# Stretches of scores exchanged and the split of the score maxima moved to GpSimd, in a float32 attention and feed-forward kernel

## The chip, the cores and the metric

The kernel runs on one core of one Trainium2 chip. The metric is the device time of one execution in microseconds (us); less is better. Engines: PE (TensorE), DVE (VectorE), ACT (ScalarE), POOL (GpSimd), SP (SyncE, which here issues nearly all DMAs).

## The reference

Two sequences of T = 1024 rows of D = 512 pass attention with 32 query heads and 8 key/value heads of 16 columns, a layer norm, a gated feed-forward layer with 1408 hidden columns, and a second layer norm, in float32:

```python
Q, K = _rope(x @ Wq.T + bq), _rope(x @ Wk.T + bk); V = x @ Wv.T + bv   # by heads
w = softmax(einsum('bhqd,bhkd->bhqk', Q, K) / sqrt(16))
x = _layernorm(x + einsum('bhqk,bhkd->bhqd', w, V) @ Wo.T + bo)
hdn = silu((x @ gate_w.T) * gate_s) * ((x @ up_w.T) * up_s)
x = _layernorm(x + (hdn @ down_w.T) * down_s)
```

## The kernel before

The main loop runs over iterations u, written (n, v) with u = 16n + v. n is one of 16 pairs of batch and key/value head, v counts 2 halves of the queries (qh) times 8 tiles of 128 keys (kt). A group is the 8 iterations of one n and qh. In each iteration the four query heads g of the key/value head have their scores computed for 128 keys and 512 queries (`scores`, L448, PE into one of three PSUM banks PS2), ACT takes the exponential of each (`exponent`, L756), and one iteration later `weigh` (L467) multiplies the exponentials with the values into the bank PV, eight matmuls on four column groups. A bank of PS2 is free when its exponential is done. After 8 iterations ACT copies PV to SBUF (`finish`, L765) and SP sends it to DRAM (L1524); the next group's first `weigh` waits for that copy.

Behind each score PE issues half a step of the running maxima for a later group (`maxima_half`, L426, on other rows of the array than the score), into one of two slots of two banks in PSA. DVE reduces them (`maximum`): for g = 2 and 3 both halves at once (L964, 128x1024), for g = 0 and 1 half by half (L957, L960). Two steps fall to one iteration. With the last of a group's 16 steps, in iteration 3 or 11 of an n, `turn_max` runs four small instructions on DVE: join of the halves (L973), a rounded copy (L977), the remainder (L979), a 32x32 transposition (L984). SP's `write_max` waits for it, writes the result to DRAM (`mscr`, L1511), waits for that to land, and reads it back as two more rows of the operand Qt (L1514). The first score of the group 5 iterations later waits for this read.

`weigh(u - 1)` comes after g = 2 in even iterations and after g = 3 in odd ones. So five scores lie between two of them, then three. The first score behind the `weigh` of an even iteration (c % 8 == 3) is split into pieces of 128 and 384 columns.

Other work is tied to iteration numbers by tables: `project_at` (projection of one 128-row block of Q or K, 24 matmuls, L365), `values_at`, `out_at` (output projection, L493), each after the scores of an odd iteration, 11 in all, in the two banks that `free_banks` names; `rope_end` (ACT rounds one half, L748, POOL subtracts, L1286, SP writes the block out); `recip_at` (DVE reciprocal L990, SP writes it, L1541, and, when that has landed, reads it back spread over partitions, 512 KB, `Bn<-rscr`, L1547, then POOL multiplies, L1330); `gather_at` (the twelve DMAs that fetch Qt and Kt of head n + 2). Every engine runs its own program in order; SP takes in iteration u first `write_max`, then `finish`, `swap_halves` (L1477, L1478), the reciprocal's two transfers, and later entries. Those of `recip_at` at (2, 11), (4, 11), (6, 3), (8, 3) and (10, 3) share their iteration with a turn of the maxima. The last 12 iterations and the feed-forward layer follow in `feed_forward`.

## Time and profile before

| what | value |
|---|---|
| runs, median of 3 | 1063.52 us (1063.1 to 1064.48) |
| profiled execution | 1064.13 us, its span 1062.3 us |
| PE busy | 1026.5 us (97%), granted clock 0.998 |
| DVE, ACT, POOL busy | 809.5, 665.1, 266.2 us |
| exponentials (L756) | 1146, mean 559 ns |
| maxima (L964, L960, L957) | 256 each, mean 1219, 682, 681 ns |

The span runs from the first to the last instruction of the program; the execution's own time has 1.8 us around it. Times in the rows below are counted from the start of the span. Mean durations overlap the next instruction's start, so what an instruction costs its engine is read from start to start. A digit of busy share says little here, because the end of a matmul is modelled.

### The profile page before, as it was taken

Reading aid. Unit: us, or ns where it says so; the run is one execution under the profiler, and the core shown is the slowest. Engines: PE = TensorE matmul, PEld = TensorE weight load, DVE = VectorE, ACT = ScalarE, POOL = GpSimd, SP = SyncE. Lnnn points to the kernel's source line nnn. Section 1 sums busy time; section 2 is a strip of 40 time slices with the busy share of each in tenths; the row PEclk is TensorE's granted clock in tenths of the full one; section 3 lists DMA queues with packets and bytes.
Section 4 is the critical chain, followed back from the end, with each engine's and each line's share of the span. In section 5 each row is a group of like instructions: output and inputs, shape, how many; then the busy total and the mean of one; then the engine's idle time right before and its main releaser. Section 6 shows DMA issues by size and latency. Waiting matters only on the chain.

```text
span 1062.3 us, 15699 instructions
## 1 busy us (share of the span) xinstructions
PE 1026.5 (97%) x5858; PEld 536.8 (51%) x5858; DVE 809.5 (76%) x1199; ACT 665.1 (63%) x1346; POOL 266.2 (25%) x227
## 2 busy tenths in 40 slices
PE   8999999999999999999999999999999999999996
PEld 3643344433443433443444443333337888888885
DVE  4899978899779799779988899999803475662535
ACT  2368877788778788778766678888863431222221
POOL 2751030141335422246200042844100000000002
PEclk9999999999999999999999999999999999999999
DMA  5274417243142512344140446531217510402011
GB/s 200 80 196 126 106 35 213 52 97 78 52 115 75 105 56 54 82 108 105 34 78 12 116 120 150 124 121 37 93 68 193 166 40 9 111 28 52 1 39 42
DMA packets 64432, 94.87 MB, mean 89 GB/s; under 512 B 37536, under 2 KB 37920, under 8 KB 62272
## 3 DMA queue, kind: packets, MB, share of 16 engines
q1 hardware_dynamic: 63776, 93.10, 33.2%
q8 instruction: 48, 0.79, 0.3%
q10 hardware_dynamic: 576, 0.72, 0.2%
q14 instruction: 32, 0.26, 0.1%
HBM read 53.95 MB, written 27.00 MB: 76 GB/s over the span
## 4 chain that ended last, share of the span: by engine, by line
PE 80%; DVE 10%; ACT 6%; issue 2%; DMA 1%; SPq 0%; POOL 0%; DVEq 0%; POOLq 0%
PE PS L448 21%; PE PV L467 20%; PE PSA L537 15%; PE PS L554 5%; PE PSA L426 5%; DVE nmx L964 5%; PE PS L365 4%; ACT Bn L756 3%; PE PS L493 2%; PE PSA L493 2%; DVE nmx L960 2%; DVE nmx L957 2%; ACT Bn L765 2%; PE PV L554 2%; PE PSA L365 1%
## 5 line engine op out<-in xcount | busy, mean ns | idle before, releaser
L756 ACT ACTIVATE Bn<-PS 128x512 f32<-128x512 f32 x1146 | 548.8, 559 | 125.0 <-PE PS L448 111.1
L448 PE MATMUL PS<-Qt,Kt 50*128 50x512 f32 x1146 | 391.7, 434 | 20.0 <-ACT Bn L756 18.7
L426 PE MATMUL PSA<-Kt,Qt 48*128 48x512 f32 x1024 | 390.0, 459 | 2.2 <-DVE Kt L936 0.8
L964 DVE TENSOR_REDUCE nmx<-PSA 128x1 f32<-128x1024 f32 x256 | 312.2, 1219 | 61.0 <-PE PSA L426 59.8
L448 PEld LDWEIGHTS PS<-Qt,Kt 50*128 50x128 f32 x1146 | 184.4, 184 | 323.6 <-ACT Bn L756 312.7
L467 PE MATMUL PV<-Bn 128*32 128x512 f32 x2048 | 272.8, 605 | 0.0
L426 PEld LDWEIGHTS PSA<-Kt,Qt 48*128 48x128 f32 x1024 | 174.6, 183 | 21.7 <-DVE nmx L964 6.2
L960 DVE TENSOR_REDUCE nmx<-PSA 128x1 f32<-128x512 f32 x256 | 174.5, 682 | 1.4 <-PE PSA L426 1.1
L957 DVE TENSOR_REDUCE nmx<-PSA 128x1 f32<-128x512 f32 x256 | 174.3, 681 | 0.0
L537 PE MATMUL PSA<-x1Th,wr 128*128 128x512 f32 x344 | 135.0, 393 | 0.8 <-DVE sg L1052 0.5
L537 PE MATMUL PSA<-x1Tl,wr 128*128 128x512 f32 x344 | 134.7, 392 | 0.0
L1052 DVE SCALAR_TENSOR_TENSOR sg<-PSA,us,sg 128x512 f32<-128x512 f32 x43 | 32.1, 749 | 103.8 <-ACT sg L792 103.8
L792 ACT ACTIVATE sg<-PSA,gs 128x512 f32<-128x512 f32 x43 | 29.6, 690 | 128.3 <-PE PSA L537 128.2
L467 PEld LDWEIGHTS PV<-Bn 128*32 128x32 f32 x2048 | 40.3, 108 | 75.8 <-issue 75.8
L537 PEld LDWEIGHTS PSA<-x1Th,wr 128*128 128x128 f32 x344 | 64.6, 188 | 16.9 <-issue 1.8
L537 PEld LDWEIGHTS PSA<-x1Tl,wr 128*128 128x128 f32 x344 | 64.6, 188 | 14.8 <-issue 1.5
L1351 POOL TENSOR_SCALAR ve<-mv 128x2 f32<-128x2 f32 (+1 forms) x11 | 2.9, 260 | 263.9 <-DVE mv L999 263.9
L1278 POOL TENSOR_TENSOR A<-A 128x1024 f32<-128x1024 f32 x8 | 19.1, 2382 | 174.4 <-DMA A<-A 172.6
L1330 POOL TENSOR_TENSOR Bn<-Bn 128x1024 f32<-128x1024 f32 x8 | 19.1, 2385 | 148.4 <-DMA Bn<-rscr 148.4
L1072 DVE TENSOR_TENSOR hTl<-sg,hTh 128x512 fp32r<-128x512 f32 x38 | 26.3, 693 | 31.8 <-ACT hTh L805 31.8
L805 ACT CAST hTh<-sg 128x512 fp32r<-128x512 f32 x38 | 23.6, 621 | 42.8 <-DVE sg L1052 36.8
L554 PE MATMUL PS<-wr,hTh 128*128 128x512 f32 x114 | 44.6, 391 | 0.0
(166 smaller groups left out, 919.4 us busy)
## 6 DMA issues: line engine op xcount, KB each, us to landing
Qt<-pscr SPq DMA_DIRECT2D x90, 128.0 KB, 4.9
A<-in_wf SPq DMA_DIRECT2D x11, 768.0 KB, 6.3
wr<-A SPq DMA_DIRECT2D x33, 256.0 KB, 2.9
pscr<-A SPq DMA_DIRECT2D x16, 512.0 KB, 3.7
vscr<-Bn SPq DMA_DIRECT2D x32, 256.0 KB, 2.0
Kt<-pscr SPq DMA_DIRECT2D x90, 64.0 KB, 2.3
A<-A SPq DMA_DIRECT2D x16, 256.0 KB, 3.7
Bn<-vscr SPq DMA_DIRECT2D x8, 512.0 KB
```

The lines of the kernel that those rows point to most:

```text
L365: op = e.matmul(ps, v, t, start=first and i == 0, stop=last and end)
L426: op = e.matmul(PSA[:, 2 * s + h, :], Qt[n % 3][p:p + NC_, g % 2, 128 * qt:128 * qt + 128], Kt[n % 3][p:p + NC_, 512 * h:512 * h + 512], s ...
L448: e.matmul(PS2[:, i, cols], Kt[n % 3][rows, 128 * kt:128 * kt + 128], Qt[n % 3][rows, g % 2, 512 * qh + cols.start:512 * qh + cols.stop], ...
L467: op = e.matmul(PV[32 * g:32 * g + 32, :], Bn[:, o:o + 32], Pb[c % NP_], start=(kt == 0), stop=(kt == 7), tile_position=(0, 32 * g))
L493: op = e.matmul(ps, t_, v, start=(k == 0 and i == 0), stop=(k == KT - 1 and i == len(pairs) - 1))
L537: op = e.matmul(gate_bank(x, q, j), v, t, start=(k == 0 and m == 0), stop=(k == KT - 1 and m == (1 if x else 0)))
L554: op = e.matmul(bank(t), v, t_, start=(i == 0 and m == 0), stop=(i == FI - 1 and end))
L756: e.activation(Pb[c % NP_][:, cols], PS2[:, score_bank[c, p], cols], ACT.Exp, scale=0.25).then_inc(*act_exp.next(piece(c, p)))
L957: e.tensor_reduce(nmx[:, hh % 2, 16 + c0:17 + c0], slot_pair(s)[:, 0, :], AX.X, ALU.max, negate=True).then_inc(*dve_max[s].next((k, 0)))
L960: e.tensor_reduce(nmx[:, hh % 2, c0:c0 + 1], slot_pair(s)[:, 1, :], AX.X, ALU.max, negate=True).then_inc(*dve_max[s].next(k))
L964: e.tensor_reduce(nmx[:, hh % 2, c0:c0 + 1], slot_pair(s), AX.XY, ALU.max, negate=True).then_inc(*dve_max[s].next(k))
L1052: e.scalar_tensor_tensor(out=out, in0=gate_bank(x, q, 1), scalar=us[:, i:i + 1], in1=sg[q % 2], op0=ALU.mult, op1=ALU.mult).then_inc(*dve_ ...
```

## The change

The order of `weigh` is exchanged: after g = 3 in even iterations and after g = 2 in odd ones, and the split score moves with it to c % 8 == 7. Projection, value and output stages now follow directly on the `weigh` of an odd iteration, ahead of its fourth score; ACT's evacuations and DVE's additions are put at the same place in their programs. For groups 1 to 30 (`apart`) DVE keeps the join, POOL does the rounded copy and the remainder (`split_max`), and DVE transposes after the first maximum of the next group. SP writes the maxima in iteration 4 of 8 instead of 3, behind what it issues in iteration 3. The fetch of head n + 2 moves from (n, 3) to (n, 5), and the roundings come 7 and 9 iterations after a projection instead of 6 and 7.

```diff
--- before.py
+++ after.py
@@ -250,6 +250,7 @@
         dve_gate, dve_h, dve_x, dve_z = count("dve_gate"), count("dve_h"), count("dve_x"), count("dve_z")
         dve_out, dve_turn, dve_parts = count("dve_out"), count("dve_turn"), count("dve_parts")
 
+        pool_ms = count("pool_ms")
         pool_one, pool_cs, pool_rope = count("pool_one"), count("pool_cs"), count("pool_rope")
         pool_split, pool_xb, pool_at = count("pool_split"), count("pool_xb"), count("pool_at")
         pool_low, pool_ve, pool_add = count("pool_low"), count("pool_ve"), count("pool_add")
@@ -262,15 +263,15 @@
         jobs = [(0, 1), (0, 2), (0, 3), (1, 4), (1, 0), (1, 1), (1, 2), (1, 3)]
         project_at = {(1, 11): 2, (4, 11): 3, (5, 3): 4, (6, 3): 5, (8, 3): 6, (8, 11): 7}
         rope_end = {(0, 1): (0, "h0"), (0, 2): (0, "h1"), (0, 3): (0, "out"),
-                    (0, 4): (1, "rope"), (0, 7): (1, "h0"), (0, 9): (1, "h1"), (0, 10): (1, "out")}
+                    (0, 4): (1, "rope"), (0, 8): (1, "h0"), (0, 10): (1, "h1"), (0, 11): (1, "out")}
         for at_u, j in project_at.items():
-            u0 = 16 * at_u[0] + at_u[1] + 6
-            rope_end.update({divmod(u0, 16): (j, "h0"), divmod(u0 + 1, 16): (j, "h1"), divmod(u0 + 2, 16): (j, "out")})
+            u0 = 16 * at_u[0] + at_u[1] + 7
+            rope_end.update({divmod(u0, 16): (j, "h0"), divmod(u0 + 2, 16): (j, "h1"), divmod(u0 + 3, 16): (j, "out")})
         values_at = (2, 11)
         out_at = {(10, 3): 0, (10, 11): 1, (11, 3): 2, (11, 11): 3}
         norm_at = {(10, 11): 0, (11, 3): 1, (11, 11): 2}
         recip_at = {(2, 11): 0, (4, 11): 1, (6, 3): 2, (8, 3): 3, (10, 3): 4, (12, 6): 5, (14, 6): 6}
-        gather_at = {(n, {0: 13, 6: 5}.get(n, 3)): n + 2 for n in range(NG - 2)}
+        gather_at = {(n, {0: 13}.get(n, 5)): n + 2 for n in range(NG - 2)}
         x_at = {(part // 2, 8 * (part % 2)): (0, part) for part in range(4)}
         x_at.update({(2 + part // 2, 5 + 8 * (part % 2)): (1, part) for part in range(4)})
         ffn_at, low_at = {}, {}
@@ -286,12 +287,19 @@
 
             return stream[k][2] < 2
 
+        def apart(hh):
+
+            return 1 <= hh < 2 * NG - 1
+
+        def low_max(hh):
+            return (pool_ms if apart(hh) else dve_ms).at(("low", hh))
+
         def slot_pair(s):
             return PSA[:, 2 * s:2 * s + 2, :]
 
         def pieces(c):
 
-            return [slice(0, 128), slice(128, 512)] if c % 8 == 3 and c < 4 * SPLIT else [slice(0, 512)]
+            return [slice(0, 128), slice(128, 512)] if c % 8 == 7 and c < 4 * SPLIT else [slice(0, 512)]
 
         score_bank = {}
         for c in range(4 * U):
@@ -302,7 +310,7 @@
             return c if p == len(pieces(c)) - 1 else (c, p)
 
         def free_banks(u):
-            last = score_bank[4 * u + 3, len(pieces(4 * u + 3)) - 1]
+            last = score_bank[4 * u + 2, 0]
             return (last + 1) % 3, last
 
         def ffn_slots(x):
@@ -663,6 +671,20 @@
                     project_half(1, 0, 0, (1, 2, 3))
                 else:
                     project_half(1, 1, 3, ((0, 1), (2, 3))[k - 2])
+            def background(u):
+                at_u, pair = divmod(u, 16), free_banks(u)
+                if at_u in project_at:
+                    for h, i in enumerate(pair):
+                        project_half(project_at[at_u], h, i, (0, 1, 2, 3))
+                if at_u == values_at:
+                    for t in range(8):
+                        value_rows(1, t, pair[t // 4])
+                if at_u in out_at:
+                    t2 = out_at[at_u]
+                    out_project(False, 0, t2, [bank(i) for i in pair], [bank_free[i] for i in pair])
+                    for j, i in enumerate(pair):
+                        bank_free[i] = dve_y.at((False, 0, 2 * t2 + j))
+
             for u in range(SPLIT):
                 at_u = divmod(u, 16)
                 for g in range(4):
@@ -670,19 +692,9 @@
                     advance(1)
                     if len(pieces(4 * u + g)) == 2:
                         scores(u, g, 1)
-                    if u >= 1 and g == (2, 3)[u % 2]:
+                    if u >= 1 and g == (3, 2)[u % 2]:
                         weigh(u - 1)
-                if at_u in project_at:
-                    for h, i in enumerate(free_banks(u)):
-                        project_half(project_at[at_u], h, i, (0, 1, 2, 3))
-                if at_u == values_at:
-                    for t in range(8):
-                        value_rows(1, t, free_banks(u)[t // 4])
-                if at_u in out_at:
-                    t2, pair = out_at[at_u], free_banks(u)
-                    out_project(False, 0, t2, [bank(i) for i in pair], [bank_free[i] for i in pair])
-                    for j, i in enumerate(pair):
-                        bank_free[i] = dve_y.at((False, 0, 2 * t2 + j))
+                        background(u)
                 if at_u == (15, 1):
                     flag_sum()
                 if at_u == (15, 2):
@@ -892,11 +904,11 @@
                 at_u = divmod(u, 16)
                 for g in range(4):
                     exponent(u, g)
+                    if g == 2 and at_u in project_at:
+                        for h, i in enumerate(free_banks(u)):
+                            evacuate_raw(project_at[at_u], h, i)
                 if u >= 1:
                     finish(u - 1)
-                if at_u in project_at:
-                    for h, i in enumerate(free_banks(u)):
-                        evacuate_raw(project_at[at_u], h, i)
                 if at_u in rope_end and rope_end[at_u][1] in ("h0", "h1"):
                     round_half(rope_end[at_u][0], int(rope_end[at_u][1] == "h1"))
                 if at_u == (15, 2):
@@ -944,33 +956,40 @@
                     bv[:, :].rearrange("p (o v c) -> p o v c", o=1, v=NKV).to_broadcast([128, 4, NKV, HD]),
                     ALU.add).then_inc(*dve_val.next((b, h)))
 
-            def maximum(k):
+            def maximum(k, halves=(0, 1)):
                 if k >= len(stream):
                     return
                 s, hh = slot_of(k), k // 16
                 g, qt = stream[k][2], stream[k][1]
                 c0 = 4 * g + qt % 4
                 if hh >= 2:
-                    w.wait_ge(*dve_ms.at(("low", hh - 2)))
+                    w.wait_ge(*low_max(hh - 2))
                 if by_halves(k):
-                    w.wait_ge(*pe_max.at((k, 0)))
-                    e.tensor_reduce(nmx[:, hh % 2, 16 + c0:17 + c0], slot_pair(s)[:, 0, :], AX.X, ALU.max, negate=True).then_inc(
-                        *dve_max[s].next((k, 0)))
-                    w.wait_ge(*pe_max.at(k))
-                    e.tensor_reduce(nmx[:, hh % 2, c0:c0 + 1], slot_pair(s)[:, 1, :], AX.X, ALU.max, negate=True).then_inc(
-                        *dve_max[s].next(k))
+                    for h in halves:
+                        w.wait_ge(*pe_max.at((k, 0) if h == 0 else k))
+                        col = nmx[:, hh % 2, c0 + 16 * (h == 0):c0 + 16 * (h == 0) + 1]
+                        e.tensor_reduce(col, slot_pair(s)[:, h, :], AX.X, ALU.max, negate=True).then_inc(
+                            *dve_max[s].next((k, 0) if h == 0 else k))
                 else:
                     w.wait_ge(*pe_max.at(k))
                     e.tensor_reduce(nmx[:, hh % 2, c0:c0 + 1], slot_pair(s), AX.XY, ALU.max, negate=True).then_inc(
                         *dve_max[s].next(k))
-                if k % 16 == 15:
-                    turn_max(hh)
-
-            def turn_max(hh):
+                if 1 in halves and k % 16 == 15:
+                    join_max(hh)
+                    if not apart(hh):
+                        split_max(hh)
+                        turn_max(hh)
+                if k % 16 == 0 and k > 16 and apart(hh - 1):
+                    turn_max(hh - 1)
+
+            def join_max(hh):
                 top, rest = nmx[:, hh % 2, 0:16], nmx[:, hh % 2, 16:24]
                 for k in (16 * hh + 14, 16 * hh + 15):
                     w.wait_ge(*dve_max[slot_of(k)].at(k))
                 e.tensor_tensor(top[:, 0:8], top[:, 0:8], rest, ALU.min).then_inc(*dve_ms.next(("join", hh)))
+
+            def split_max(hh):
+                top = nmx[:, hh % 2, 0:16]
                 w.wait_ge(*dve_ms.at(("join", hh)))
                 if hh >= 1:
                     w.wait_ge(*dve_ms.at(("turn", hh - 1)))
@@ -978,7 +997,9 @@
                 w.wait_ge(*dve_ms.at(("high", hh)))
                 e.tensor_tensor(msp[:, 16:32], top, msp[:, 0:16].bitcast(F32), ALU.subtract).then_inc(
                     *dve_ms.next(("low", hh)))
-                w.wait_ge(*dve_ms.at(("low", hh)))
+
+            def turn_max(hh):
+                w.wait_ge(*low_max(hh))
                 if hh >= 2:
                     w.wait_ge(*max_out[hh % 2].at(hh - 2))
                 e.transpose(mrow[:, hh % 2, :], msp[:, :].bitcast(F32)).then_inc(*dve_ms.next(("turn", hh)))
@@ -1216,14 +1237,19 @@
             for u in range(SPLIT):
                 at_u = divmod(u, 16)
                 maximum(next(steps))
-                maximum(next(steps))
-                if at_u in norm_at:
-                    first_norm(False, 0, norm_at[at_u])
-                if at_u == values_at:
-                    for h, i in enumerate(free_banks(u)):
-                        add_values(1, h, i)
-                if at_u in out_at:
-                    add_rows(False, 0, out_at[at_u], [bank(i) for i in free_banks(u)])
+                k = next(steps)
+                if at_u in norm_at or at_u in out_at or at_u == values_at:
+                    maximum(k, (0,))
+                    if at_u in norm_at:
+                        first_norm(False, 0, norm_at[at_u])
+                    if at_u == values_at:
+                        for h, i in enumerate(free_banks(u)):
+                            add_values(1, h, i)
+                    if at_u in out_at:
+                        add_rows(False, 0, out_at[at_u], [bank(i) for i in free_banks(u)])
+                    maximum(k, (1,))
+                else:
+                    maximum(k)
                 if at_u in recip_at:
                     reciprocal(recip_at[at_u])
                 if at_u == (15, 0):
@@ -1266,6 +1292,15 @@
                     w.wait_ge(*act_split.at(("x0", h, k)))
                     e.tensor_tensor(xl0[j][:, :], xT[:, h, k, :], xh0[j][:, :].bitcast(F32), ALU.subtract).then_inc(
                         *pool_split.next(("x0", h, k)))
+
+            def split_max(hh):
+                top = nmx[:, hh % 2, 0:16]
+                w.wait_ge(*dve_ms.at(("join", hh)))
+                w.wait_ge(*dve_ms.at(("turn", hh - 1)))
+                e.tensor_copy(msp[:, 0:16], top).then_inc(*pool_ms.next(("high", hh)))
+                w.wait_ge(*pool_ms.at(("high", hh)))
+                e.tensor_tensor(msp[:, 16:32], top, msp[:, 0:16].bitcast(F32), ALU.subtract).then_inc(
+                    *pool_ms.next(("low", hh)))
 
             def rope(j):
                 b, m = jobs[j]
@@ -1410,6 +1445,8 @@
                 at_u = divmod(u, 16)
                 if at_u in norm_at:
                     spread_of(2, (False, 0, norm_at[at_u]))
+                if u % 8 == 3 and apart(steps_done(u) // 16 - 1):
+                    split_max(steps_done(u) // 16 - 1)
                 if at_u in project_at:
                     rope(project_at[at_u])
                 if at_u in recip_at:
@@ -1653,8 +1690,10 @@
             swap_halves(1)
             for u in range(SPLIT):
                 at_u = divmod(u, 16)
-                if steps_done(u) // 16 > steps_done(u - 1) // 16:
+                if u % 8 == 4:
                     write_max(steps_done(u) // 16 - 1)
+                if u == SPLIT - 1:
+                    write_max(2 * NG - 1)
                 if u >= 1:
                     finish(u - 1)
                 if at_u in project_at:
```

## Rows read from the trace of the kernel before

**Rows 1.** the page's part 4, the chain that ended last, by engine

```profile
PE 80%; DVE 10%; ACT 6%; issue 2%; DMA 1%; SPq 0%; POOL 0%; DVEq 0%; POOLq 0%
```

**Rows 2.** timeline of PE, two periods (start us, length us, engine, line, operation, count)

```profile
221.08 1.06 PE L467 MATMUL PV<-Bn 128*32 128x512 f32 x8
...
224.61 1.06 PE L467 MATMUL PV<-Bn 128*32 128x512 f32 x8
...
226.50 1.06 PE L467 MATMUL PV<-Bn 128*32 128x512 f32 x8
...
229.55 1.06 PE L467 MATMUL PV<-Bn 128*32 128x512 f32 x8
...
231.44 1.06 PE L467 MATMUL PV<-Bn 128*32 128x512 f32 x8
...
234.90 0.64 PE L467 MATMUL PV<-Bn 128*32 128x512 f32 x4
```

**Rows 3.** timeline of ACT, same stretch (in brackets: idle before it, releaser)

```profile
223.04 0.58 ACT L765 COPY Bn<-PV 128x512 f32<-128x512 f32 x1
...
226.14 4.40 ACT L756 ACTIVATE Bn<-PS 128x512 f32<-128x512 f32 x9 [0.54 <-PE PS L448]
```

**Rows 4.** timeline of DVE, around one turn of the maxima

```profile
228.75 1.23 DVE L964 TENSOR_REDUCE nmx<-PSA 128x1 f32<-128x1024 f32 x1
...
230.49 0.68 DVE L960 TENSOR_REDUCE nmx<-PSA 128x1 f32<-128x512 f32 x1
231.28 0.17 DVE L973 TENSOR_TENSOR nmx<-nmx 128x8 f32<-128x8 f32 x1
...
232.03 1.18 DVE L964 TENSOR_REDUCE nmx<-PSA 128x1 f32<-128x1024 f32 x1
```

**Rows 5.** timeline of ACT, two roundings of a half

```profile
67.68 0.64 ACT L748 CAST A<-A 128x512 fp32r<-128x512 f32 x1
...
70.68 0.61 ACT L748 CAST A<-A 128x512 fp32r<-128x512 f32 x1
```

**Rows 6.** timeline of all engines, copy of PV in the tail

```profile
772.70 1.06 PE L467 MATMUL PV<-Bn 128*32 128x512 f32 x8
...
773.83 0.59 ACT L765 COPY Bn<-PV 128x512 f32<-128x512 f32 x1 [0.43 <-PE PV L467]
774.31 1.09 ACT L756 ACTIVATE Bn<-PS 128x512 f32<-128x512 f32 x2
```

**Rows 7.** groups of instructions on GpSimd (count | busy us, mean ns | idle before)

```profile
L1291 POOL TENSOR_TENSOR xl<-A,xh 128x512 fp32r<-128x512 f32 x8 | 10.3, 1284 | 0.6
...
L1351 POOL TENSOR_SCALAR ve<-mv 128x2 f32<-128x2 f32 x2 | 0.5, 237 | 35.4 <-DVE mv L999 35.4
```

**Rows 8.** timeline of PE, end of a projection stage

```profile
277.29 0.39 PE L365 MATMUL PS<-xl,wh 128*128 128x512 f32 x1
...
278.88 1.06 PE L467 MATMUL PV<-Bn 128*32 128x512 f32 x8
```

**Rows 9.** timeline of SP's issues, iterations (4, 11) and after

```profile
273.43 0.57 SPq L1511 DMA_DIRECT2D mscr<-mrow  x1
275.41 0.54 SPq L1514 DMA_DIRECT2D Qt<-mscr  x2
...
279.64 0.59 SPq L1541 DMA_DIRECT2D rscr<-rn  x1
282.86 0.66 SPq L1547 DMA_DIRECT2D Bn<-rscr  x1
```

**Rows 10.** busy time by stretch (each engine, PE clock, DMA share, GB/s)

```profile
285.00:287.00 2.00, 2.00 (x15) 0.97 (x19) 2.00 (x3) 1.85 (x6) 2.00 (x2) 1.00 0.51 147
288.50:289.50 1.00, 1.00 (x12) 0.16 (x8) 0.84 (x2) 1.00 (x3) 1.00 (x1) 1.00 0.02 8
```

**Rows 11.** timeline of SP's issues, the latest read of the maxima

```profile
656.51 0.56 SPq L1511 DMA_DIRECT2D mscr<-mrow  x1
662.81 0.56 SPq L1514 DMA_DIRECT2D Qt<-mscr  x2
```

## The prediction

> **What bounds the kernel now.** I read the page first. PE looks busy nearly all the time, and the chain of waits puts 80% of the span on PE, 10% on DVE and 6% on ACT [rows 1]. That is no proof that PE is the limit, because matmul ends are modelled. So I went to PE's timeline in a quiet piece of the attention loop, and read the starts of the value product (L467, called W here; eight matmuls, about 1.0 us until the next one can start) [rows 2]. They alternate. From W at 224.61 to W at 226.50 is a short stretch of 1.89 us (three scores), from 226.50 to 229.55 a long one of 3.05 us (five scores, the first in two pieces). Two iterations take 4.94 us.
>
> In ACT's view [rows 3] nine exponentials run without a gap for 4.40 us, and ACT idles 0.54 us ahead of them, which is where W has kept PE from giving it a score. In the long stretch PE waits for banks that ACT empties, so work put on ACT there costs its full time. In the gap behind the long stretch's W, ACT has 0.54 us to give away. DVE [rows 4] starts a whole-pair maximum at 228.75 and the second half maximum after it at 230.49. With 0.60 us to whatever may follow, one iteration of maxima is 2.34 us and two are 4.68, which leaves 0.26 us of slack. ACT sets the pace, with DVE close behind.
>
> Three kinds of place depart from 4.94:
> - Copy of PV (L765), once in eight iterations, in the long stretch: 221.08 to 224.61 is 3.53 us, 0.48 more [rows 2, 3]. The loop has 30 such stretches of 3.53 or 3.54.
> - Four small DVE instructions (L973 to L984): the next maximum starts at 232.03 instead of 230.49 + 0.60 = 231.09, 0.94 us late. The long stretch of that moment, 231.44 to 234.90, has 3.46 us, 0.41 more [rows 2, 4]. There are 14 of these. The others lie beside a projection stage, or behind a stretch in which DVE had caught up, and cost nothing.
> - Rounding a half (L748): at 67.68 it lies in ACT's gap and costs nothing. At 70.68 it lies between exponentials of a long stretch and costs about 0.5 [rows 5]. Seven lie so.
>
> **The change, part by part.** *Exchange of stretches.* By itself it is a shift by one iteration, so 4.94 stays. What is tied to iteration numbers moves against it. The copy of PV stays at the end of iteration 8m, which now is where the long stretch's W ends, in ACT's gap. The nearest row is in the tail, where the copy waits for its W: W 772.70, copy 773.83, next exponential 774.31 [rows 6]. So the exponential comes at W + 1.61, where ACT's gap ends at W + 1.53 (229.55 to 231.08, the start behind the nine, 226.14 + 4.40 + 0.54). Those 0.08 us vanish in the 0.15 that ACT idles ahead of the split score. Gain: 30 x 0.48 = **14.4 us**. The next W needs the copy's end at W + 1.72 and comes at W + 1.89: 0.17 to spare.
>
> *Roundings.* Both halves now fall behind even iterations, in the gap. Two keep a cost: (0, 1), now in a long stretch, and (0, 8), which meets the copy. From seven to two: 5 x 0.5 = **2.5 us**.
>
> *Maxima.* DVE keeps the join and the transposition. The join still waits for the last maximum: 231.28 - 230.49 = 0.79, then about 0.13 to an instruction that doesn't depend on it, less the 0.60 of before: 0.32. The transposition comes a maximum later, when nothing is left to wait for: 0.13 [rows 4]. So DVE loses 0.45 instead of 0.94 us, in two parts. Against 0.26 of slack in two iterations it is caught up in the next two. Followed maximum by maximum, the slots come free 0.01 to 0.05 us ahead of the matmuls that want them. So most of 14 x 0.41 = **5.7 us** is gained, and I take back **1.0** for these thin margins (bounds 0 and 30 x 0.41 = 12.3, if every turn stalls as the 14 did).
>
> *The split on GpSimd.* No row has 16 columns. The bounds are 0.24 us (128x2) and 1.28 (128x512) for each of the two [rows 7]. I take 0.3, as both are nearly all start-up, plus two semaphores: ready 0.7 us after the join. The transposition comes 1.14 + 0.1 after it, the length of a whole-pair maximum, so this is hidden. GpSimd's long work (the rotation, the splits of x, w and A, the low parts) starts behind the split in program order and takes at most some 15 us of the 19.8 between two splits. [...]
>
> *Projection, value and output stages*, 11 of them, go between W and the split score. Before, last product 277.29 to W 278.88 is 1.59, and a long stretch of 3.05 follows [rows 8]: 4.64. After, a short stretch of 1.89 precedes the stage, and behind it the second evacuation, the two-piece score, three exponentials and four scores take about 2.8 us to W: 4.7. I cost it at nothing. DVE's last half maximum and the join now come behind the stage, but its next maximum waits for PE anyway.
>
> *Rows fetched later.* The twelve issues of a gather go from iteration 3 to 5, behind the write of the maxima, still 14 iterations ahead of their use: nothing.
>
> *Write of the maxima.* This is what speaks against the change. SP's write (L1511) goes from iteration 8m+3 to 8m+4, and so is moved past everything that SP issues at 8m+3. Normally it is issued at 273.43, read back from 275.41 [rows 9], and the read has about 1.5 us more to land, by an estimate from the write's own 1.98, of which it has half the bytes; with 0.3 for the second issue that makes 3.8 us. The new turn leaves 7.3 us to the first score that needs it (8.7 before), so it is hidden in ordinary groups. In five groups, however, the reciprocal's write and the broadcast read RB (L1547, 512 KB) stand at 8m+3 as well. Count from the last product of the stage, E = 277.29. The reciprocal is written at E + 2.35 (279.64), and RB is issued at E + 5.57 (282.86) [rows 8, 9]. Now the write of the maxima follows, at E + 6.2. RB keeps half of the DMA engines busy (share 0.51 at 285 to 287) and is over by 288.5 to 289 (0.02 left) [rows 10]. That small writes wait for large transfers issued ahead is in the trace: the write at 656.51 lets its read go only at 662.81, 6.3 us instead of 1.98 [rows 9, 11]. So it lands near E + 12, and the maxima near E + 13.9. PE wants them at 2.8 + 4.94 + 1.9 + 1.3 = E + 10.9: PE stands for 3.0 us, of which a fuller ring of banks gives 0.1 back. That is three groups, (4,11), (6,3), (8,3): **8.7 us**. At (2,11) and (10,3) no swap of halves delays the reciprocal's write and RB goes out 1.5 us sooner: 2 x 1.3 = **2.6**. The group of the late write at 656.51 had only 0.5 us left, and its transfers don't speed up while PE does by 1.6: **1.1**. Sum 12.4; bounds 0 (the write isn't held up) and 18 (RB as slow as with a gather beside it, 2 us more in three).
>
> The Trainium skill (DMA: Bandwidth & Descriptors, Why a DMA increments its semaphore by 16 and not by 1, and Queues, rings and completion order) says that such a transfer uses only the k lowest-numbered engines and that each consumes descriptors in ring order. The half share agrees. By that rule the case half way in rival 1 is the right one.
>
> **Sum.** -14.4 - 2.5 - 5.7 + 1.0 + 12.4 = -9.2. The profiled execution has 1064.1 us (span 1062.3 and 1.8 around it), which gives 1054.9. The median of the runs is 0.6 lower, so 1063.5 - 9.2 = **1054.3 us**.
>
> **Rivals.**
> 1. *The write isn't held up* (other engines, or RB drains sooner). For it: I know its engines by no row. Against: 656.51. Without the 12.4: 1042; with a third of it, 1046. Chance 0.17. Half way lies the case in which the write waits for its own few engines alone: one us less in each of five groups gives 1050, the lower end of my own range, and has 0.15 of the chance of my forecast.
> 2. *DVE becomes the limit at each turn.* For it: margins of hundredths. Against: 0.45 of added work, not 0.94. If half of the 12.3 comes: 1060. The same size follows if W has to wait 0.2 us for the copy of PV in 30 places. Chance 0.14.
> 3. *Slower: GpSimd is late.* The upper bound for the pair is 2.6 us. If it costs 2.0, the transposition holds DVE for 0.8 us, and what is beyond its slack, about 0.6, stops PE in 30 groups: +18, so 1072. It decides once the pair takes over 1.24 + 0.25 + 0.3 = 1.8 us. Chance 0.08.
> 4. *Gains and stalls cancel* (copy saves half, stalls at their upper bound): 1063. Chance 0.06.
>
> My forecast has 0.55, with 1050 to 1059 as its own range. The range 1044 to 1061 takes in most of 1 and 2 and leaves the rest. A difference under 0.2% (2 us) is about what a measurement of this kernel can't tell from none. Faster 0.85, within 0.2% 0.06, slower 0.09.
>
> **What the profile will show.** Right: L765 behind a gap on ACT at W + 1.1, and no stretch of 3.5 left; L748 behind it; the transposition between two maxima with no gap; GpSimd's pair under 0.7 us; and in five groups SP's L1511 straight behind L1547, its read 5 to 6 us later, and PE standing some 3 us at the first score of the next group. Wrong: the write of the maxima taking 2 us even there (rival 1), long stretches of 3.2 or more behind each turn (2), or DVE idle ahead of the transposition with GpSimd as releaser (3).

## The result, and the profile after

| kernel | median | runs |
|---|---|---|
| before | 1063.37 us | 4 |
| after | 1077.07 us (1074.61 to 1079.0) | 4 |

The changed kernel is slower: ratio 1.0126, 95% interval 1.0103 to 1.0148. The forecast was 1054.3 us with a range of 1044 to 1061 and 0.09 for slower; the time lies 22.8 us above it and outside the range. The profiled execution of after took 1077.6 us, span 1075.7, granted clock 0.98.

Begin with what came as forecast. PE's timeline of after, at the place of [rows 2]; W is now L475:

```profile
218.48 1.06 PE L475 MATMUL PV<-Bn 128*32 128x512 f32 x8
...
221.52 1.07 PE L475 MATMUL PV<-Bn 128*32 128x512 f32 x8
...
223.41 1.07 PE L475 MATMUL PV<-Bn 128*32 128x512 f32 x8
...
226.45 1.06 PE L475 MATMUL PV<-Bn 128*32 128x512 f32 x8
```

The steps are 3.04, 1.89 and 3.04. The stretch of 3.53 is gone, although the copy of PV lies right here. ACT's timeline shows why, against [rows 3]:

```profile
218.12 4.39 ACT L768 ACTIVATE Bn<-PS 128x512 f32<-128x512 f32 x9 [0.54 <-PE PS L456]
222.65 0.59 ACT L777 COPY Bn<-PV 128x512 f32<-128x512 f32 x1
223.13 4.30 ACT L768 ACTIVATE Bn<-PS 128x512 f32<-128x512 f32 x9
```

The copy starts at 222.65, 1.13 behind W at 221.52, in the gap that ACT had there, and the nine exponentials behind it follow without a gap. The turn of the maxima, in the timelines of DVE and of GpSimd (POOL), against [rows 4]:

```profile
230.77 0.17 DVE L989 TENSOR_TENSOR nmx<-nmx 128x8 f32<-128x8 f32 x1
230.86 1.22 DVE L975 TENSOR_REDUCE nmx<-PSA 128x1 f32<-128x1024 f32 x1
231.99 0.20 DVE L1005 STREAM_TRANSPOSE mrow<-msp 128x32 f32<-128x32 f32 x1
```

```profile
231.00 0.20 POOL L1300 CAST msp<-nmx 128x16 fp32r<-128x16 f32 x1 [10.35 <-DVE nmx L989]
231.28 0.22 POOL L1302 TENSOR_TENSOR msp<-nmx,msp 128x16 fp32r<-128x16 f32 x1
```

GpSimd is done at 231.50, 0.5 us ahead of the transposition, which stands between two maxima with no idle time. In heads 1 to 14 no stretch of 3.46, 3.53 or 3.56 is left in after; the only longer ones lie in projection, value and output stages and in the six places below.

What went wrong shows first in the chain of waits by engine, against [rows 1]. DVE and ACT, 16% before, have nearly left it, and transfers have come in:

```profile
PE 85%; DMA 8%; DVE 3%; ACT 1%; SPq 1%; issue 1%; POOL 0%; DVEq 0%; POOLq 0%
```

Then in PE's waits, by releaser (line waited for: us in total, times, longest):

```profile
PE PS L456 <- DMA Qt<-mscr: 15.2, 5, 4.0
PE PSA L434 <- DVE nmx L971: 7.2, 1, 7.2
```

The five are the five groups of the forecast: 2.63 us at 199.03, 3.01 at 288.48, 4.00 at 366.55, 4.04 at 458.35, 1.54 at 552.48. SP's issues around the second, against [rows 9]:

```profile
276.67 0.59 SPq L1578 DMA_DIRECT2D rscr<-rn  x1
279.89 0.64 SPq L1584 DMA_DIRECT2D Bn<-rscr  x1
280.62 0.58 SPq L1548 DMA_DIRECT2D mscr<-mrow  x1
286.25 0.57 SPq L1551 DMA_DIRECT2D Qt<-mscr  x2
```

The write of the maxima stands straight behind the read RB, and its own read goes 5.63 us later instead of 1.98 (5.63 to 6.25 in the five groups). The forecast had 5 to 6. What it did not have stands at each wait. PE's timeline:

```profile
288.48 0.76 PE L456 MATMUL PS<-Qt,Kt 50*128 50x512 f32 x1 [3.01 <-DMA Qt<-mscr]
...
290.66 1.93 PE L475 MATMUL PV<-Bn 128*32 128x512 f32 x8
...
294.10 1.37 PE L475 MATMUL PV<-Bn 128*32 128x512 f32 x8
...
297.45 1.06 PE L475 MATMUL PV<-Bn 128*32 128x512 f32 x8
```

and the busy time by stretch (columns as in [rows 10], the third number from the end is PE's granted clock):

```profile
199.20:202.60 3.40, 3.40 (x16) 1.09 (x15) 2.42 (x3) 2.07 (x4) 0.00 (x0) 0.50 0.29 111
288.00:294.80 6.80, 6.32 (x26) 2.41 (x30) 3.41 (x4) 4.11 (x8) 1.30 (x1) 0.50 0.10 38
366.50:373.20 6.70, 6.65 (x30) 2.41 (x30) 3.75 (x5) 4.24 (x8) 2.08 (x3) 0.50 0.89 164
458.60:462.00 3.40, 3.40 (x16) 0.92 (x14) 2.42 (x3) 2.08 (x4) 0.00 (x0) 0.50 0.66 162
554.20:557.60 3.40, 3.40 (x18) 1.00 (x16) 1.91 (x4) 2.34 (x5) 0.00 (x0) 0.50 1.03 174
666.90:680.40 13.50, 8.39 (x34) 3.09 (x34) 6.22 (x9) 3.16 (x7) 11.25 (x13) 0.50 0.35 108
```

Six stretches at 0.50, which is 1.2 instead of 2.4 GHz, one at each pause of PE. Two begin up to 0.3 us behind the end of the wait and one 1.7 us behind it; at 288, 366 and 667 the clock was already down before PE went on. Eight matmuls of W take 1.93 us instead of 1.06, and 294.10 - 290.66 = 3.44 and 297.45 - 294.10 = 3.35 stand where 1.89 and 3.05 belong. Adding the surplus of the W steps in each of the five groups gives 3.9, 5.55, 6.75, 5.3 and 3.1: 24.6 us, of which the waits themselves are 15.2. Before had no such stretch inside the loops.

The sixth was not in the forecast at all. All engines around it:

```profile
660.88 0.61 SPq L1584 DMA_DIRECT2D Bn<-rscr  x1
...
662.25 0.17 DVE L989 TENSOR_TENSOR nmx<-nmx 128x8 f32<-128x8 f32 x1
...
668.35 2.34 POOL L1365 TENSOR_TENSOR Bn<-Bn 128x1024 f32<-128x1024 f32 x1 [17.94 <-DMA Bn<-rscr]
...
670.63 0.20 POOL L1300 CAST msp<-nmx 128x16 fp32r<-128x16 f32 x1
670.91 0.22 POOL L1302 TENSOR_TENSOR msp<-nmx,msp 128x16 fp32r<-128x16 f32 x1
...
671.17 0.21 DVE L1005 STREAM_TRANSPOSE mrow<-msp 128x32 f32<-128x32 f32 x1 [7.62 <-POOL msp L1302]
...
672.01 0.79 PE L434 MATMUL PSA<-Kt,Qt 48*128 48x512 f32 x1 [7.18 <-DVE nmx L971]
```

Read it backwards. PE waits 7.18 us for DVE to empty a slot; DVE waits 7.62 us in the transposition for GpSimd's split; the split, whose join was done at 662.4, stands in GpSimd's program behind the divide of (12, 6), L1365; and the divide waits for RB, which was issued at 660.88, 6.87 us behind the reciprocal's write at 654.01. Before, no turn of the maxima went through GpSimd (inside the loops DVE waited for it only in the layer norm, 1.2 us at a time), and the same lateness cost nothing. The steps around it are 9.87, 4.55 and 3.35 instead of 1.89, 3.05 and 1.89: 10.9 us.

### The profile page after: what moved, and what is told of

Its sections match the earlier page's. It is cut to its first block, busy times and chain, and to the rows that moved or that the text cites. A ratio compares the mean times of both kernels' runs of the same rounds, so it can differ in the third digit from the quotient of the medians.

```text
span 1075.7 us, 15699 instructions
## 1 busy us (share of the span) xinstructions
PE 1032.2 (96%) x5858; PEld 538.8 (50%) x5858; DVE 796.2 (74%) x1139; ACT 667.2 (62%) x1346; POOL 278.2 (26%) x287
## 4 chain that ended last, share of the span: by engine, by line
PE 85%; DMA 8%; DVE 3%; ACT 1%; SPq 1%; issue 1%; POOL 0%; DVEq 0%; POOLq 0%
PE PS L456 26%; PE PV L475 21%; PE PSA L545 14%; PE PS L562 5%; PE PSA L434 5%; PE PS L373 4%; DMA mscr<-mrow 3%; PE PS L501 2%; PE PSA L501 2%; DMA rscr<-rn 2%; PE PSA L373 2%; PE PV L562 1%; PE PS L415 1%; DVE nmx L971 1%; DMA Qt<-mscr 1%; DMA wr<-A 1%
## 5 line engine op out<-in xcount | busy, mean ns | idle before, releaser
L456 PE MATMUL PS<-Qt,Kt 50*128 50x512 f32 x1146 | 396.2, 441 | 22.0 <-DMA Qt<-mscr 15.2
L456 PEld LDWEIGHTS PS<-Qt,Kt 50*128 50x128 f32 x1146 | 189.1, 187 | 335.8 <-ACT Bn L768 294.6
L971 DVE TENSOR_REDUCE nmx<-PSA 128x1 f32<-128x512 f32 x512 | 327.8, 680 | 35.2 <-PE PSA L434 35.2
L475 PE MATMUL PV<-Bn 128*32 128x512 f32 x2048 | 279.5, 618 | 0.0
L434 PEld LDWEIGHTS PSA<-Kt,Qt 48*128 48x128 f32 x1024 | 177.9, 187 | 19.7 <-DVE nmx L971 10.9
L475 PEld LDWEIGHTS PV<-Bn 128*32 128x32 f32 x2048 | 40.7, 109 | 77.7 <-issue 67.7
L1300 POOL CAST msp<-nmx 128x16 fp32r<-128x16 f32 x30 | 5.9, 198 | 265.6 <-DVE nmx L989 265.6
L545 PEld LDWEIGHTS PSA<-x1Th,wr 128*128 128x128 f32 x344 | 64.6, 188 | 16.9 <-issue 1.8
L562 PE MATMUL PS<-wr,hTl 128*128 128x512 f32 x114 | 44.5, 390 | 0.0
L1365 POOL TENSOR_TENSOR Bn<-Bn 128x1024 f32<-128x1024 f32 x8 | 18.8, 2355 | 94.3 <-DMA Bn<-rscr 94.3
```

The source lines that it names most:

```text
L434: op = e.matmul(PSA[:, 2 * s + h, :], Qt[n % 3][p:p + NC_, g % 2, 128 * qt:128 * qt + 128], Kt[n % 3][p:p + NC_, 512 * h:512 * h + 512], s ...
L456: e.matmul(PS2[:, i, cols], Kt[n % 3][rows, 128 * kt:128 * kt + 128], Qt[n % 3][rows, g % 2, 512 * qh + cols.start:512 * qh + cols.stop], ...
L475: op = e.matmul(PV[32 * g:32 * g + 32, :], Bn[:, o:o + 32], Pb[c % NP_], start=(kt == 0), stop=(kt == 7), tile_position=(0, 32 * g))
L545: op = e.matmul(gate_bank(x, q, j), v, t, start=(k == 0 and m == 0), stop=(k == KT - 1 and m == (1 if x else 0)))
L562: op = e.matmul(bank(t), v, t_, start=(i == 0 and m == 0), stop=(i == FI - 1 and end))
L971: e.tensor_reduce(col, slot_pair(s)[:, h, :], AX.X, ALU.max, negate=True).then_inc(*dve_max[s].next((k, 0) if h == 0 else k))
```

## Experiments

Each was timed against before on the same chip, and the ratios are to that. "After" is 1077.07 us throughout; the medians of before were 1064.11 us beside e1 to e4, 1063.71 beside e5 to e8 and 1063.44 beside e9 and e10, 1063.37 beside after, so differences to after can be off by 0.7 us. Step means the distance between two starts of W, and is named by the iteration (n, v) whose exponentials the first of them weighs.

**e1_recip_behind.** The reciprocal's write and RB one iteration later, behind the write of the maxima.

```diff
                 if u == SPLIT - 1:
                     write_max(2 * NG - 1)
+                if divmod(u - 1, 16) in recip_at:
+                    write_reciprocal(recip_at[divmod(u - 1, 16)])
+                    read_reciprocal(recip_at[divmod(u - 1, 16)])
...
-                if at_u in recip_at:
-                    write_reciprocal(recip_at[at_u])
-                    read_reciprocal(recip_at[at_u])
```

> The changed kernel with SP's two transfers of the reciprocal issued one iteration later, behind the write of the maxima; everything else as in the changed kernel. Queue theory: in the five groups where these transfers stood ahead of the write, the wait of PE on the maxima (2.6, 3.0, 4.0, 4.0 and 1.5 us) and the slow stretch behind it disappear, together 24.6 us of the intervals between value products; the stop at iteration 204 of 7.2 us stays: 1052 us. Rival, the transfers only collide elsewhere (the broadcast read now delays something else by as much): over 1065. Rival, the loss lies in the exchange of the stretches or in GpSimd's part and not in SP's order: 1077.

Measured: 1052.79 us, ratio 0.9897 (0.988 to 0.9913). All five waits are gone and so are the five half-clock stretches: 24.3 us, where the trace of after had 24.6. The late stop stays, 7.24 us at 646.90 with 13.65 us at half clock about it. The kernel is now 10.6 us faster than before, so the order of these transfers alone decided the sign.

**e2_divide_behind.** GpSimd's divides of (12, 6) and (14, 6) five iterations later, behind the next split.

```diff
-                if at_u in recip_at:
+                if at_u in recip_at and recip_at[at_u] < 5:
                     divide(recip_at[at_u])
+                if divmod(u - 5, 16) in recip_at and recip_at[divmod(u - 5, 16)] >= 5:
+                    divide(recip_at[divmod(u - 5, 16)])
```

> The changed kernel with GpSimd's multiplications of the sixth and seventh block by the reciprocals moved from iterations (12, 6) and (14, 6) to (12, 11) and (14, 11), behind the split of the maxima. Queue theory: the stop of 7.2 us, in which DVE's transposition waited for a split that stood behind a multiplication that waited for a DMA, disappears with its slow stretch, 10.9 us in all; the five other waits stay: 1066 us. Rival, GpSimd's split is late for another reason (low parts of the weights): 1077.

Measured: 1069.83 us, 1.006 (1.0042 to 1.0078), a gain of 7.2 over after. The stop at (12, 11) is gone, which settles its cause. Of the 10.9 us, 2.5 came back: now PE meets the late read of the maxima at (12, 14), 2.43 us, where the step is 5.56. The five waits are of much the same size (1.39 to 3.81), but the half-clock stretches about them were 6.83, 10.24, 10.24, 6.83 and none, more than in after, and the wait of 2.43 had none.

**e3_both_behind.** Both edits.

```diff
+                    divide(recip_at[divmod(u - 5, 16)])
...
+                    write_reciprocal(recip_at[divmod(u - 1, 16)])
+                    read_reciprocal(recip_at[divmod(u - 1, 16)])
```

> Both moves together. Queue theory: the losses add, 24.6 + 10.9 us are gone and only the gains of the exchange, of the roundings and of the turn are left: 1041.6 us, some 22 us under the kernel before. Rival, the two losses are not independent (one hides behind the other): 1046 or more.

Measured: 1044.74 us, 0.9825 (0.9809 to 0.9842). Two surpluses are left: 2.1 at (12, 14), a wait of 2.01 on the read of the maxima, and 0.95 at (6, 11), where the divide, at 358.45 late by its RB, shifts GpSimd's low part into the join. In the profiled execution the clock never falls in the loops.

**e4_filled_wait.** After, with 12, 14, 18, 18 and 7 additional score matmuls (their result is overwritten) ahead of the first score of the five groups, so that PE works while the maxima are in flight.

```diff
                 if g == 0 and u in (48, 80, 104, 136, 168):
+                    for _ in range({48: 12, 80: 14, 104: 18, 136: 18, 168: 7}[u]):
+                        e.matmul(PS2[:, i, cols], Kt[n % 3][0:NC_, 128 * kt:128 * kt + 128],
+                                 Qt[n % 3][0:NC_, 0, 512 * qh:512 * qh + 512], start=True, stop=True)
```

> The changed kernel with 12, 14, 18, 18 and 7 additional score matmuls ahead of the first score of the five groups that wait for their maxima, written to the bank that the real score overwrites; PE works where it would stand, and the write of the maxima is as late as before. Clock theory: PE is granted half the clock for 3.4 to 6.8 us only because it had stood still, which is 24.6 - 15.2 = 9.4 us of the loss; with the wait filled the clock stays up, and about 8 of them come back: 1069 us, the low stretches behind these five gone and the one at iteration 204 still there. Rival, the slow stretches come from the restart of the pipeline of banks and exponentials, or the low clock from something that doesn't depend on PE's pause: 1077.

Measured: 1070.84 us, 1.0073 (1.0044 to 1.0102), 6.2 less than after. At the third to fifth group the clock stays full: 7.0, 1.89 and 3.05 instead of 7.72, 3.44 and 3.58 at the third. The surplus left at these three is 3.95, 3.94 and 1.41 us, the waits of after were 4.00, 4.04 and 1.54: with the clock full a late read costs its wait and no more. Behind the first two 3.41 us at half clock remain. So the loss beside the waits came with the clock, and part of it was bought back here.

**e8_filled_more.** The same with more of them.

```diff
-                    for _ in range({48: 12, 80: 14, 104: 18, 136: 18, 168: 7}[u]):
+                    for _ in range({48: 16, 80: 18, 104: 20, 136: 20, 168: 9}[u]):
```

> As the version with the filled waits, with 16, 18, 20, 20 and 9 additional matmuls instead of 12, 14, 18, 18 and 7. There the clock still fell for 3.4 us behind the first two waits. If what was left of PE's pause (0.3 us and the time until the banks are full again) did that, more matmuls take it away, and the stretches behind the first two become 1.89 and 3.05: 2 us less, against up to 0.9 us more of filling at each: 1069 to 1072. Rival, the low clock there has to do with how little the additional matmuls use of the array, so it stays: 1072 to 1074.

Measured: 1074.57 us, 1.0108 (1.0062 to 1.0154). The clock stays full at the first, third and fifth group (steps 6.51 and 1.88 at the first), but falls at the second and fourth (8.54, 3.44, 4.23 and 8.49, 3.44, 3.41). The intervals of e4 and e8 overlap, so which is faster is not shown, but more filling did not mean more clock, against the theory. What exactly lets it fall stays open.

**e5_exchange_alone.** After, with all turns on DVE as before, and SP's write in iteration 3 of 8.

```diff
         def apart(hh):
-            return 1 <= hh < 2 * NG - 1
+            return False
...
-                if u % 8 == 4:
+                if u % 8 == 3:
                     write_max(steps_done(u) // 16 - 1)
-                if u == SPLIT - 1:
-                    write_max(2 * NG - 1)
```

> The changed kernel with the maxima's part taken out: DVE runs join, rounded copy, remainder and transposition in one go, and SP writes the maxima in iteration 3 of 8, ahead of all else; exchange of the stretches, places of the stages and roundings as in the changed kernel. Queue theory: no wait on the maxima in the five groups and none at iteration 204; of the gains 14.4 (copies) and 2.5 (roundings) stay, and the turn now costs 0.4 us in all 20 groups without a stage, because DVE no longer catches up behind the copies: 1063.4 - 16.9 + 2.5 = 1049, with a wait of about 1 us at (12, 12) 1050. Rival, the exchange itself is not worth its 14.4 because DVE becomes the limit everywhere: 1056 or more.

Measured: 1064.46 us over 10 runs, 0.9996 (0.9983 to 1.0009): no change, and 15 us above what I expected. Two things were missing in my sum. A turn on DVE now falls into a short step, which becomes 2.40 instead of 1.89, in nearly every group (26 turns add 12.1 us to the steps of e9), while before only 14 of them cost something. And there were three new stops. At (12, 14) a late read cost 2.6 us, 0.98 of them wait. At (5, 14) PE waited 3.80 us: SP's issues show that the write of the maxima stood behind the rows of head 7 (Qt<-pscr) and took 5.52 us until its read:

```profile
322.64 4.35 SPq L1539 DMA_DIRECT2D Qt<-pscr  x6
327.04 0.41 SPq L1561 DMA_DIRECT2D vscr<-Bn  x1
327.56 0.59 SPq L1548 DMA_DIRECT2D mscr<-mrow  x1
333.08 0.54 SPq L1551 DMA_DIRECT2D Qt<-mscr  x2
```

At (6, 11) PE waited 2.77 us for DVE, with 10.24 us at half clock about it. DVE's and GpSimd's timelines:

```profile
374.26 0.92 DVE L989 TENSOR_TENSOR nmx<-nmx 128x8 f32<-128x8 f32 x1
375.21 1.21 DVE L996 CAST msp<-nmx 128x16 fp32r<-128x16 f32 x1
376.45 1.27 DVE L998 TENSOR_TENSOR msp<-nmx,msp 128x16 fp32r<-128x16 f32 x1
```

```profile
373.88 1.28 POOL L1326 TENSOR_TENSOR wl<-A,wh 128x512 fp32r<-128x512 f32 x1
375.11 2.58 POOL L1321 TENSOR_TENSOR A<-A 128x512 f32<-128x512 f32 x2
```

The join L989 takes 0.17 us in after, as its like L973 does before [rows 4]. Here the three small instructions end at 375.18, 376.42 and 377.72, and GpSimd's three at 375.16, about 376.4 and 377.69. The ends fall together within 0.03 us, so each instruction of DVE was held by the one beside it.

**e6_both_and_load.** Both edits of e3, all divides behind the next split, and the sixth load of the late weights five iterations later.

```diff
-            ffn_at.setdefault(divmod(11 * 16 + 5 + 8 * (i // 2) + 3 * (i % 2), 16), []).append(i)
+            ffn_at.setdefault(divmod(11 * 16 + 5 + 8 * (i // 2) + (8 if i == 5 else 3 * (i % 2)), 16), []).append(i)
...
-                if at_u in recip_at:
-                    divide(recip_at[at_u])
+                for back in (5, 8):
+                    kc = recip_at.get(divmod(u - back, 16), -1)
+                    if kc >= 0 and (kc >= 5) == (back == 5):
+                        divide(kc)
```

> The version with both moves, and two more: every multiplication by the reciprocals goes to GpSimd behind the next split, and the sixth load of feed-forward weights is issued 5 iterations later, behind the write of the maxima. Queue theory: the two late stretches that were left (5.12 instead of 3.05 us at (12, 14), 2.84 instead of 1.89 at (6, 11)) become ordinary: 3.0 us under that version, 1041.7. Rival, the stretch at (12, 14) waits for something else than the write behind that load: 1043.5 or more.

Measured: 1042.96 us, 0.9804 (0.9787 to 0.982). The two surpluses of e3 are gone. One of 0.8 appeared at (5, 14).

**e7_maxima_alone.** Before, with only the split on GpSimd, the transposition one maximum later and SP's write in iteration 4, and with e6's places for the reciprocal, the divides and the load. The fetch of head n + 2 stands at (n, 5), as in after. The exchange and the later roundings are left out.

```diff
-                    turn_max(hh)
+                    join_max(hh)
+                    if not apart(hh):
+                        split_max(hh)
+                        turn_max(hh)
+                if k % 16 == 0 and k > 16 and apart(hh - 1):
+                    turn_max(hh - 1)
```

> The kernel before with only the maxima's part (join on DVE, split on GpSimd, transposition one maximum later, write in iteration 4), with the reciprocal's transfers, the multiplications and the sixth weight load behind it; the stretches are not exchanged. Theory: the 14 stretches of 3.46 us become 3.05, those with a copy of PV (3.53) and with a rounding (3.56) stay: 1063.4 - 5.7 = 1057.7. Rival, the turn was hidden only because the exchange put it elsewhere, and costs the same here: 1063.

Measured: 1057.42 us, 0.9943 (0.9926 to 0.9959). Every step of 3.46 became 3.05, those of 3.53 and 3.56 stayed, and nothing new came. So the maxima's part is worth 6.0 us without the exchange; the forecast had 5.7.

**e9_rows_behind.** e6, with the rows of head 7 fetched behind the write of the maxima.

```diff
-        gather_at = {(n, {0: 13}.get(n, 5)): n + 2 for n in range(NG - 2)}
+        gather_at = {(n, {0: 13, 5: 13}.get(n, 5)): n + 2 for n in range(NG - 2)}
```

> The version with everything late put behind (both_and_load), and head 7's rows fetched at (5,13) instead of (5,5). Theory: the write of maxima of (5,12) landed 4.01 us after its issue at 321.96, because the six transfers of Qt<-pscr issued from 317.42 still ran until 325.24; with the fetch behind the write it lands after some 1.4 us, the stretch of 3.85 us at (5,14) becomes 3.05, and no other grows: 1042.2 us (0.8 less). Rival: the fetch of head 7 is now late for its own first use, or the rope stores at (5,13) hold it up: a new wait of 1 us or more at (6,x), 1043 to 1047 us.

Measured: 1041.62 us (1040.44 to 1043.27), 0.9797 (0.9784 to 0.9811). The step at (5, 14) is 3.04. Its median is the lowest, 21.8 us below before and 35.4 below after; e6's lies within its spread, and it is the step that shows the gain. SP's issues at the place of [rows 9] show the order that e1 introduced, the maxima read after 2.01 us and RB last:

```profile
273.50 0.60 SPq L1550 DMA_DIRECT2D mscr<-mrow  x1
275.51 0.54 SPq L1553 DMA_DIRECT2D Qt<-mscr  x2
276.10 0.34 SPq L1580 DMA_DIRECT2D rscr<-rn  x1
277.62 0.66 SPq L1586 DMA_DIRECT2D Bn<-rscr  x1
```

**e10_turn_on_dve.** e9, with e5's edit.

```diff
         def apart(hh):
-            return 1 <= hh < 2 * NG - 1
+            return False
```

> The same kernel, but with the maxima of every head split and turned on DVE at once and written by SP in iteration 3 of 8 (GpSimd has no part in it). Theory: exchange_alone missed its 1049 us for two reasons: each turn lengthens a short stretch, 1.89 to 2.40 us (some 24 of them, 12.2 us in its trace), and three late steps with half the clock behind them (15 us) that the later transfers take away. So here only the turns remain: 1042.2 + 12.2 = 1054.4 us, PE never at half clock before the end, short stretches of 2.40 at iterations 3 and 11. Rival: the DVE turn beside GpSimd's long instructions (the three small ones took 3.7 us at 374.26 in exchange_alone) makes new waits of its own: over 1057 us and a wait of PE on DVE of over 1 us.

Measured: 1058.56 us, 0.9946 (0.9931 to 0.9961), 4 us over my figure and with a stop that my rival named. In the trace, 25 turns add 11.9 us in all, about as counted beforehand. (6, 11) adds 1.2, and a stop at (10, 10) 3.9; together 17.0, and the profiled executions differ by 17.3. The stop, in the timelines of GpSimd, DVE and PE:

```profile
551.86 2.40 POOL L1365 TENSOR_TENSOR Bn<-Bn 128x1024 f32<-128x1024 f32 x1
...
551.92 3.08 DVE L1025 TENSOR_SCALAR x1a<-x1a,mv,ve 128x512 f32<-128x512 f32 x2 [1.17 <-POOL ve L1388]
...
555.65 0.32 PE L456 MATMUL PS<-Qt,Kt 50*128 50x128 f32 x1 [1.30 <-DVE x1a L1041]
```

In e9 the split keeps the divide away from this place, and the same two instructions take 1.00:

```profile
541.82 1.00 DVE L1025 TENSOR_SCALAR x1a<-x1a,mv,ve 128x512 f32<-128x512 f32 x2 [1.17 <-POOL ve L1388]
```

Behind the wait of 1.30 us PE had half clock for 6.83 us, from 556.82. In e3 a wait of 2.01 us, at 648.59, left it full.

## Why the prediction was wrong

1. *Exchange of stretches and roundings, -14.4 and -2.5.* Right, beside the split. e9 less e7 is -15.8; the two terms make -16.9. But the first steps of the last head went from 2.43, 3.04 and 3.1 to 3.61, 1.94 and 4.0, and cost 1.0, for which I had no term; e7, without the exchange, keeps the old ones. The eleven stages, costed at nothing, cost 0.01 to 0.08 us each. Without the split the exchange is worth less: e10, which has everything of e9 but the maxima's part, is 4.9 us under before: turns on DVE lengthen the short steps by 11.9 us and bring stops of 5.1. The two parts alone give 4.9 and 6.0 us and together 21.8, so they are not independent terms of a sum, as mine had them; the sum held only since both were made.
2. *Maxima, -5.7.* Right: -6.0 in e7. The 1.0 that I took back for thin margins did not come; nowhere did DVE stop PE at a turn in time. The sum of the gains was forecast at -21.6; e9 has -21.8. That they agree so closely is in part luck: the 1.0 taken back here stood in for the 1.0 of the last head.
3. *The split on GpSimd.* Its two instructions take 0.20 and 0.22 us, a little under the lower bound of 0.24, so rival 3 as I wrote it was wrong. The step that failed is the sentence behind it: "GpSimd's long work ... starts behind the split in program order and takes at most some 15 us of the 19.8". I added up what GpSimd computes and left out what it waits for. The divide of (12, 6) waits for a transfer, and before the change no turn of the maxima waited for GpSimd. Cost 10.9 us where I had 1.1 for this group. e2 showed it, and with the stop gone the late read that the 1.1 stood for cost 2.5 us (2.1 in e3). This is rival 3's mechanism with another releaser, and it could be read from before:

```profile
653.33 0.61 SPq L1547 DMA_DIRECT2D Bn<-rscr  x1
...
655.65 0.17 DVE L973 TENSOR_TENSOR nmx<-nmx 128x8 f32<-128x8 f32 x1
...
660.67 2.38 POOL L1330 TENSOR_TENSOR Bn<-Bn 128x1024 f32<-128x1024 f32 x1 [18.24 <-DMA Bn<-rscr]
```

   The join is done at 655.82, and the divide, which stands ahead of the next split, ends at 663.05.
4. *Write of the maxima, 8.7 + 2.6.* Place and mechanism were right, and the waits were a third longer than forecast, 15.2 us where I had 11.3: 3.01, 4.00 and 4.04 us where I had 2.9 each, 2.63 and 1.54 where I had 1.3 each. The case half way in rival 1, one us less in each group, did not come. The failed step is that I priced a pause of PE by its length alone. The five groups lost 24.6 us (24.3 in e1). The other 9.4 us came with PE's clock, half at each wait, and my sum had no term for it.

The account closes: -21.6 + 24.6 + 10.9 = +13.9, measured +13.7. Of the miss of 22.8, 13.3 lie in the five groups and 9.8 in the late one (together 23.1).

The Trainium skill (TensorE: Matmul & The Clock Gate, HAM oscillation — how this bites in real kernels) tells of a kernel in which a wait for data between two runs of matmuls puts the next ones at half clock, each time. This trace agrees: five waits for a DMA, five stretches at 0.50. The length of a wait alone does not decide it: 2.01 us left the clock full in e3 and 2.43 in e2, while 1.30 us went with half clock in e10 and 0.98 in e5.

## What to carry to other kernels

When an engine that the critical path did not wait for is given a small step of the critical path, list every instruction ahead of that step in its program and what each waits for, DMAs first: its lateness was free before and is not any more. A small transfer that PE needs goes ahead of any large one on the same queue; here this order alone was worth 24 us. And a pause of TensorE can cost more than its length: 15.2 us of waits cost 24.6 in after, while 2.01 us in e3 cost 2.1. Last, two edits that act on the same step are measured together and alone: here they gave 21.8 us together, 6.0 and 4.9 alone.

## What the runs showed that I had not expected

- TensorE's granted clock was half for 3.41 to 10.24 us at waits of 0.98 to 4.04 us (after, e2, e5, e10), for 13.65 us at one of 7.2 (after, e1, e4) and for 6.83 at one of 7.3 (e8). With the waits filled it still fell in some groups (e4, e8). What lets it fall is open.
- Some DVE instructions that read and write SBUF stood until the GpSimd instruction beside them ended: 0.92, 1.21 and 1.27 us instead of 0.17 (e5), 3.08 instead of 1.00 (e10). DVE's maxima, which read PSUM, kept their 1.22 us beside GpSimd's work. The Trainium skill (SBUF — State Buffer, 🔬 SBUF: two separate sides) says that GpSimd and some DVE instructions, among them those with two SBUF inputs, lock a shared pair of ports for a whole instruction. The ends that coincide within 0.03 us in e5 agree; the held cast and TENSOR_SCALAR have one such input each, the join and the remainder have two. With the split on GpSimd the cast and the remainder can't be held on DVE any more, but the join can: 1.16 us at (6, 11) in e3.
- A small write behind a large read on the same queue took 5.63 to 6.25 us until it could be read back (after), behind row fetches 5.52 (e5), and 2.0 when first (e9).
